# Slots of a graph convolution summed as fp32 column tiles instead of high and low parts, with a third set of row buffers

## The reference

```python
src, dst = (edge_index[0], edge_index[1])          # 100000 edges, sorted by dst
norm = -dinv[src] * dinv[dst]                      # dinv = rsqrt(out-degree)
def _cheb_conv(x, src, dst, norm, W0, W1, b):
    def prop(h):
        return segment_sum(h[src] * norm[:, None], dst, num_segments=x.shape[0])
    return x @ W0 + prop(x) @ W1 + b
...
h = maximum(layernorm(x), 0.0)                     # x: 6250 x 512, fp32
h = _cheb_conv(h, src, dst, norm, W1_0, W1_1, b1)
h = layer_norm(h, gamma, beta)
h = where(h >= 0, h, 0.01 * h)
out = x + _cheb_conv(h, src, dst, norm, W2_0, W2_1, b2)
```

## Time and profile before

| | |
|---|---|
| median of the runs | 2092.93 us |
| profiled execution | span 2091.0 us, from the first to the last instruction; the median lies 1.9 us above it |
| mean granted TensorE clock | 0.980 |
| busy: TensorE, VectorE, ScalarE, GpSimd | 92%, 69%, 72%, 72% |
| DMA | 514.95 MB, 246 GB/s over the span |

### The profile page before, as it was taken

The page is one execution under the profiler, slowest core; times in us unless marked ns, Lnnn a source line. Parts: engine busy times, 40 slices in busy tenths (PEclk is TensorE's granted clock), DMA queues, the critical chain, the costliest instruction groups (busy, mean ns, idle before and its releaser), DMA issues.

```text
span 2091.0 us, 25909 instructions
## 1 busy us (share of the span) xinstructions
PE 1928.9 (92%) x6822; PEld 1074.3 (51%) x6822; DVE 1438.7 (69%) x3415; ACT 1508.8 (72%) x2715; POOL 1511.5 (72%) x1596
## 2 busy tenths in 40 slices
PE   3459999999999999999997999999999999999998
PEld 3435555555555555555554555545555555555545
DVE  9857777877777777877775566655556655556554
ACT  7828788777777888777875776666667666667665
POOL 2267777777777777777777777777777777777775
PEclk9769999999999999999999999999999999999999
DMA  9888888888888888888877888888888888887886
GB/s 251 274 255 274 241 240 241 242 239 239 239 238 238 242 241 240 241 240 236 241 222 252 256 256 260 246 255 254 255 251 248 251 255 254 255 253 240 256 255 183
DMA packets 187921, 514.95 MB, mean 246 GB/s; under 512 B 44460, under 2 KB 46147, under 8 KB 186528
## 3 DMA queue, kind: packets, MB, share of 16 engines
q0 software_dynamic: 128576, 422.78, 68.9%
q1 hardware_dynamic: 56374, 90.16, 12.4%
q10 hardware_dynamic: 2828, 0.42, 0.3%
HBM read 472.40 MB, written 40.84 MB: 245 GB/s over the span
## 4 chain that ended last, share of the span: by engine, by line
PE 49%; POOL 21%; DVE 14%; issue 10%; DMA 6%; ACT 0%; SPq 0%; DVEq 0%; ACTq 0%
PE ps L1313 24%; POOL arena L589 21%; PE ps L1501 11%; PE ps L1494 6%; DMA arena<-table,idx_all 4%; PE ps L1492 4%; DVE low L1092 3%; PE ps L1305 2%; DVE ps L1162 2%; DVE w_all L895 2%; DVE stats L1165 2%; DVE ps L1172 2%; DVE work L895 1%; PE ps L1426 1%; PE ps L1424 1%
## 5 line engine op out<-in xcount | busy, mean ns | idle before, releaser
L589 POOL DMA_INDIRECT arena<-table,idx_all x1536 | 1459.0, 950 | 480.6 <-issue 441.6
L1492 PE MATMUL ps<-high,hots 128*128 128x512 f32 x1034 | 582.0, 563 | 1.4 <-ACT high L699 0.5
L1096 DVE TENSOR_TENSOR low<-arena,ps 128x512 fp32r<-128x512 f32 x517 | 348.5, 682 | 333.7 <-ACT ps L700 329.3
L1501 PE MATMUL ps<-arena,hots_full 128*128 128x512 f32 x1060 | 540.3, 602 | 30.8 <-DMA arena<-table,idx_all 30.1
L700 ACT CAST ps<-arena 128x512 fp32r<-128x512 f32 x517 | 305.1, 590 | 282.2 <-DMA arena<-table,idx_all 251.5
L1494 PE MATMUL ps<-low,hots 128*128 128x512 f32 x1034 | 417.2, 403 | 21.8 <-DVE low L1092 21.8
L1092 DVE SCALAR_TENSOR_TENSOR low<-arena,ps 128x512 fp32r<-128x512 f32 x508 | 366.0, 741 | 66.1 <-ACT ps L699 61.3
L699 ACT ACTIVATE ps<-arena 128x512 fp32r<-128x512 f32 x508 | 348.9, 687 | 31.9 <-DMA arena<-table,idx_all 31.2
L699 ACT ACTIVATE high<-arena 128x512 fp32r<-128x512 f32 x508 | 362.0, 713 | 0.0
L700 ACT CAST high<-arena 128x512 fp32r<-128x512 f32 x517 | 318.5, 616 | 0.0
L1494 PEld LDWEIGHTS ps<-low,hots 128*128 128x128 f32 x1034 | 195.3, 189 | 180.7 <-issue 92.5
(11 more groups left out here) (174 smaller groups left out, 1445.7 us busy)
## 6 DMA issues: line engine op xcount, KB each, us to landing
arena<-table SPq DMA_DIRECT2D x106, 256.0 KB
arena<-table,idx_all POOLq DMA_INDIRECT x1550, 3.9
table<-arena SPq DMA_DIRECT2D x53, 256.0 KB, 4.0
arena<-in_x_dram SPq DMA_DIRECT2D x53, 256.0 KB, 5.3
out_dram<-arena SPq DMA_DIRECT2D x53, 256.0 KB, 4.5
table<-arena SPq DMA_DIRECT2D x10, 1124.4 KB
arena<-in_x_dram POOLq DMA_DIRECT2D x9, 1120.0 KB, 35.2
w_all<-in_L_gnn_W_dram SPq DMA_DIRECT2D x2, 1024.0 KB, 14.4
```

The source lines that it names most:

```text
L589: nc.gpsimd.indirect_dma_start(out=rows[u][0:rn, c, 0:RW if L == 0 else D], out_offset=None, in_=table[L][0:NEAR if near else N, :], in_of ...
L1096: nc.vector.tensor_tensor(low[a], rows[u][:, c, 0:D], high_ps[s % NB][:, :], ALU.subtract).then_inc(s_low, 1)
L1492: nc.tensor.matmul(tx_ps[u][:, :], hot, high[a], start=c == 0, stop=False)
L1501: last = nc.tensor.matmul(tx_ps[u][:, :], hot, rows[u][:, c, 0:D], start=c == 0, stop=i >= NC - 2 and c == SLOTS - 1)
```

## The change

- `SPLIT`, `high`, `low`, `make_high`, `make_low` and the waits that go with them are gone. All slots are plain fp32.
- Each chunk but the last is summed in four strips of 32 nodes: `tx_ps[n % 2][t * 32:(t + 1) * 32]`, from the 32 columns of the hot matrix that belong to strip t. Strip t takes only the slots `STRIPS[t]` that can hold its nodes (0 to 4, 3 to 9, 7 to 13, 10 to 14). The products of different strips are issued in turn. The last chunk of a layer is summed at full width.
- `SETS = 3`: GpSimd fills a set once the chunk three before is summed (`s_tx`), with one wait per chunk.
- The order of all engines is new: a chunk's strips together, then the transposes and dense products. `slots`, `step`, `act_step` and `dve_step` are replaced by `sums`, `sums_last`, `layer_1` and `layer_2`.
- Six edges per chunk (`BOUNDS`) are tested in the prologue: one element of `dst` per slot is loaded on ScalarE's queue, and 24 operations on VectorE compare them with the strips' borders, ahead of the flag.
- SyncE loads own rows of layer 2's first chunks at the end of layer 1.

```diff
-    SPLIT = (0, 1, 4, 6, 7, 9, 10, 12, 13, 14)
...
+    Q = 32
+    STRIPS = ((0, 5), (3, 10), (7, 14), (10, SLOTS))
+    BOUNDS = ((3, False, 1), (5, True, 1), (7, False, 2), (10, True, 2), (10, False, 3), (14, True, 3))
+    ROUNDS = 7
+    SETS = 3
...
+                elif L == 0 and i <= NC - 3:
+
+                    sp.wait_ge(s_t2, i + 3)
+                    sp.wait_ge(s_tab1, 16 * 5)
+                    load_own(1, i - NC + 4)
...
+                    if n >= SETS:
+
+                        pool.wait_ge(s_tx, n - SETS + 1)
                     for c in range(slots_of(i)):
-                        if c % GW == 0 and near:
-
-                            pool.wait_ge(s_slot, summed(0, NC - 1, c + GW - 1))
-                        elif c % GW == 0 and (L or i >= 2):
-
-                            pool.wait_ge(s_slot, summed(L, i - 2, c + GW - 1))
...
+                act.dma_start(slot_edge[:, :, :],
+                              bass.AP(dst.tensor, 0, [[E, 1], [GROUP * P, K // 4], [P, GROUP]])).then_inc(s_bounds, 16)
...
+                copy_own(L, 0)
+                copy_own(L, 1)
+                for i in range(NC):
+                    take_tx(L, i)
+                    if i + 2 < NC:
+                        copy_own(L, i + 2)
+                    copy_txT(L, i)
+                    if L == 0:
+                        take_std(i)
+                        make_sloped(i, i % 2)
...
+                dve.wait_ge(s_bounds, 16)
+                chunk_begin = begin[:, 0:K].rearrange("p (g j) -> p g j", j=4)
+                for n, (c, after_it, strip) in enumerate(BOUNDS):
+                    broken = flags[:, 3 * K + 1 + n * K:3 * K + 1 + (n + 1) * K].rearrange("p (g j) -> p g j", j=4)
+                    for j in range(4):
+                        at = c + (SHORT + (j - 1) * SLOTS if j else 0)
+                        setup.add(nc.vector.scalar_tensor_tensor(
+                            out=broken[:, :, j], in0=chunk_begin[:, :, j], scalar=float(strip * Q),
+                            in1=slot_edge[:, :, at], op0=ALU.add, op1=ALU.is_gt if after_it else ALU.is_le))
...
+            def layer_1():
+                for i in range(NC):
+                    u = i % 2
+                    if i >= 2:
+
+                        dve.wait_ge(s_tx, i - 1)
+                    for c in range(slots_of(i)):
+                        one_hot(0, i, c)
+                        if c == 0 and 1 <= i <= NC - 2:
+                            hot_next(0, i - 1)
...
+                        if i and c == 9:
+                            epi = conv_stats(i - 1, 1 - u)
+                        if i and c == 11:
+                            norm1(i - 1, 1 - u, epi)
+                        if i and c == 13:
+                            finish1(i - 1, 1 - u)
...
+            def layer_2():
+                for i in range(NC):
+
+                    dve.wait_ge(s_tx, NC + i)
                     if i <= NC - 3:
...
+                        hot_next(1, i)
+                    if i + 1 < NC:
+                        for c in range(slots_of(i + 1)):
+                            one_hot(1, i + 1, c)
+                    if i:
+                        finish2(i - 1)
...
+            def strip_sum(L, i, t, c, start, stop):
+                n = L * NC + i
+                strip = slice(t * Q, (t + 1) * Q)
+                return nc.tensor.matmul(tx_ps[n % 2][strip, :], hot_of(n, c)[:, strip], rows_of(n, c)[:, 0:D],
+                                        start=start, stop=stop)
...
+                for r in range(ROUNDS):
+                    if L and i == 0 and r == 4:
+                        add_near(n % 2)
+                    for t in range(4):
+                        c0, c1 = STRIPS[t]
+                        c1 = min(c1, slots_of(i))
+                        c = c0 + r - (t == 3)
+                        if c0 <= c < c1:
+                            if c not in seen:
+                                slot_ready(L, i, c)
+                            seen.add(c)
+                            last = strip_sum(L, i, t, c, c == c0, c == c1 - 1 and not (t == 3 and follows))
+                if follows:
+
+                    pe.wait_ge(s_hotx, L * (NC - 2) + i + 1)
+                    if L:
+                        pe.wait_ge(s_gath[(n + 1) % SETS][0], landed(L, i + 1, 0))
+                    last = nc.tensor.matmul(tx_ps[n % 2][P - Q:P, :], hot_next_of(n), rows_of(n + 1, 0)[:, 0:D],
+                                            start=False, stop=True)
+                last.then_inc(s_tx, 1)
...
+                for i in range(NC):
+                    if i < NC - 1:
+                        sums(L, i)
+                    else:
+                        sums_last(L)
+                    if i + 2 < NC:
+                        transpose_own(L, i + 2)
+                    if i + 1 < NC:
+                        dense_own(L, i + 1)
+                    transpose_tx(L, i)
+                    dense_tx(L, i)
+                    if L == 0 and i in (0, 2):
+                        count_near(i // 2)
```

More of the change, by code:

```diff
@@ L126, in gnn_kernel @@
         gen_rows = arena[0:EP, at_rooms + ROOMS * D:]
[L127 to L132, removed]
+        assert at_own + 7 == ROOMS and at_rooms + ROOMS * D + RW >= NT * RW
+        hots = sb("hots", [P, 2 * SLOTS * P])
+        hots_next = sb("hots_next", [P, 2 * Q])
         w_all = sb("w_all", [P, 2 * KC * D])
@@ L301, in first_slot, with landed, hot_no, own_in @@
             return i // 4 * GROUP + (SHORT + (i % 4 - 1) * SLOTS if i % 4 else 0)
[L303 to L329, removed]
+        def landed(L, i, c):
+            n = L * NC + i
+            return 16 * sum(c < slots_of(m % NC) for m in range(n % SETS, n + 1, SETS))
+        def hot_no(L, i, c):
+            return L * S + first_slot(i) + c + 1
+        def own_in(n):
+            return sum(32 if m < NC else 16 for m in range(n % 2, n + 1, 2))
+        def strips_of(c):
+            return [t for t, (c0, c1) in enumerate(STRIPS) if c0 <= c < c1]
         def scale(i, n):
             return scal[:, bass.ds(i * NSC + n, 1)]
[L336 to L357, removed]
+        def rows_of(n, c):
+            return rows[n % SETS][:, c, :]
+        def hot_of(n, c):
+            at = (n % 2 * SLOTS + c) * P
+            return hots[:, at:at + P]
+        def hot_next_of(n):
+            return hots_next[:, n % 2 * Q:(n % 2 + 1) * Q]
         def products(i, u):
@@ L1455, in dense_own, with transpose_own @@
[L1455 to L1472 removed]
+            def transpose_own(L, i):
+                n = L * NC + i
+                pe.wait_ge(s_ownT, n)
+                pe.wait_ge(s_own[n % 2], own_in(n))
+                transposes(own_ps, own[n % 2]).then_inc(s_t2, 1)
@@ new lines, in dense_own, with dense_tx @@
+            def dense_own(L, i):
+                n = L * NC + i
+                if L and i >= 2:
+                    pe.wait_ge(s_fin, i + 1)
+                else:
+                    pe.wait_ge(s_hs1, n + 1)
+                pe.wait_ge(s_ownT, n + 1)
+                for mm, cols in products(i, n % 2):
+                    last = dense_cols(mm, cols, ownT[n % 2], weights[L][0], True, False)
+                last.then_inc(s_do, 1)
+            def dense_tx(L, i):
+                n = L * NC + i
+                pe.wait_ge(s_txT, n + 1)
+                parts = products(i, n % 2)
+                for k, (mm, cols) in enumerate(parts):
```

407 lines of the change are left out of this document (125 added, 282 removed).

## The result

The changed kernel takes 2082.61 us (2080.64 to 2083.71, 4 runs) against 2092.82 (2092.36 to 2096.65) for the kernel before in the same comparison: a ratio of 0.995, 95% interval 0.9936 to 0.9964. The profiled span went from 2091.0 to 2081.5 us, by 9.5, against the 4.6 forecast.

The account below looks back on a forecast made before the run. GpSimd's gathers, 1.25 us per slot, were taken to bound the kernel before and after. The terms -10.0 + 1.0 + 3.1 + 1.3 gave -4.6 us: span 2086.4, run 2088 us, range 2080 to 2112.

Parts of the forecast that it names:

- What bounds it: Both layers: GpSimd's gathers set the period, 1.25 us per slot, 18.44 us per chunk; TensorE second at about 17 us.
- Strips: TensorE's strip products: four run together, 0.215 us each, so TensorE needs 16 us per chunk against GpSimd's 18.44.
- Rivals 2 and 3: Strip products run in order, 2269 us (chance 0.15), or with no overlap at all, about 3400 us (chance 0.04).
- rival 2: TensorE's strip pairs run in order, 0.43 us per strip, 19.8 to 20.1 us per chunk; 2269 us, chance 0.15.
- Order in layer 1: Layer 1's loop of strips, dense work, epilogue and hots takes 17.5 to 18 us, under 18.44, not holding GpSimd.
- Third set: Start of layer 1: GpSimd's wait at 136 us for chunk 0's row buffer goes, -10.0 us.
- Prologue: Before the gathers: loading slot edges costs +1.0 us (0 to 2.5); the comparisons' 2.2 us before the flag are hidden.
- Gathers: GpSimd's gathers keep 950 ns each whether VectorE is busy or not.
- Transition: Between layers: layer 1's full-width last chunk delays the table's last store, for which GpSimd waits, +3.1 us.
- Tail: End of layer 2: the full-width last chunk's products end at 2083.4 us against 2082.1 before, +1.3 us.
- Clock: TensorE's idle of some 2.7 us per layer 1 chunk may bring 0.50 clock stretches, covered by the wait for gathers.

Follow-up runs that it names:

- experiment 4: Changed kernel with two slots of one strip, then two of the next, in place of one each; 2626.32 us where the changed kernel takes 2618 to 2628.
- Experiment 3: Changed kernel with all products of strip 0, then of strips 1, 2 and 3, instead of the strips in turn; 2807.13 us (one run).
- experiment 1: Changed kernel with two sets of row buffers instead of three; 2096.43 us, ratio 1.0021 to the kernel before.
- experiment 2: Changed kernel without the load of slot edges and the 24 comparisons; 2082.06 us, ratio 0.9954 to the kernel before.
- experiment 5: Changed kernel with all hot matrices made 128 columns wide, products reading the same 32 columns; 2087.08 us, ratio 0.998 to the kernel before.

## Why the prediction was right, step by step

- *What bounds it*: right. GpSimd's pace and slices stayed as they were, and three engines lost work without gain to the run.
- *Strips*: right. Four at once, 0.13 us per instruction: 48 of them, 24 products, took 6.2 us (experiment 4), 3.3 times as fast as at 0.86 us each. Rivals 2 and 3 fell. Experiment 3 shows that they had a mechanism: in another order, the loss of rival 2 and more comes true. The Trainium skill's rule of starts in program order (TensorE: Matmul & The Clock Gate, Part 3, The mechanism), taken strictly for these pairs, does not agree: second instructions start 0.45 us after the first, later strips' firsts 7 ns after.
- *Order in layer 1*: right. The loop was put at 17.5 to 18 us; in the changed kernel's early layer 1, before the gathers hold TensorE up, one chunk's 36 last strip instructions start 17.16 us behind the former's (163.51, 180.67), under GpSimd's 18.44.
- *Third set*: -10.0 forecast, -10.0 measured; experiment 1 gives it 13.8 in the changed kernel, with its one wait per chunk.
- *Prologue*: +1.0 forecast for the load, 0 measured (experiment 2). The flag came 2.5 us later (116.9, for 114.46 in the earlier trace rows; forecast 2.2), but it was needed earlier than at 117.7: GpSimd's queue first loads the flag, 0.5 us from 117.0 on, and only then issues the next gather. So the comparisons cost 0.7.
- *Gathers*: the step that failed. They were taken as fixed at 950 ns; narrow hot matrices made them 3.4 ns shorter each, 5.4 us in all (experiment 5). Wide ones brought 4.5 us back. This term alone is more than the forecast's error of 4.9.
- *Transition*: +3.1 forecast, +1.3 measured. The last chunk's fifteenth gather is issued at 1078.70, and TensorE ends its sums at 1087.2, 8.5 us later; before, it was 7.1.
- *Tail*: +1.3 forecast, +4.2 measured. The 13.7 us of full-width products were as forecast (2058.67 to 2072.4). What came late is all ahead of them: chunk 51's last gather started at 2042.19, landed 5.3 us later and not 3.7, and was summed from 2047.65, and the granted clock was 0.50 from 2047.83 to 2051.24, for part of the dense products at 2049.39, which took 4.62 us for 3.72.
- *Clock*: some stretches at 0.5 came, as in the earlier trace rows; only that last one is seen to cost anything; behind the others GpSimd's pauses are the usual 0.30 us.

The sum was -4.6 and the span moved by -9.5: the start right, the prologue 0.4 too dear, a gain of 5.4 not foreseen, and two errors of the last chunks, -1.8 and +2.9, that half cancel. That the time lies in the range owes something to luck. Its lower end, 2080, stood for a free prologue and cheaper last chunks; the prologue was nearly free, but the last chunks cost 1.1 us more in sum than forecast, and it was the gathers, no part of the range, that took the time to 2082.6.

## What to carry to other kernels

When an engine is off the critical path, taking work from it may still shorten the instructions of the one that is on it: read the spread of the bound engine's durations and what runs beside the long ones, not only their mean. Take apart what a change carries: here the third set of buffers was worth more than the whole gain, and the cleverer products made room for it. And products in separate column tiles overlapped fully here only where they alternated closely in the program, every one or two of a tile.

## What the runs showed of the hardware that was not expected

- Four fp32 products in four tiles of 32 columns run fully side by side, 0.86 us for a round of four pairs. With five to seven of a tile in a row it costs 0.33 us per instruction (experiment 3), with two in a row nothing (experiment 4); a tile seems to have about two products waiting while others start.
- VectorE's hot matrices beside GpSimd's gathers lengthen them, 4 to 5 us over the run for wide ones against narrow ones (experiment 5).
- One chip ran the same program 26% slower (2626.13 against 2082.61), with 540 us of pauses in front of TensorE's weight loads that wait for nothing. A gain of 0.5% on one chip was a loss of 4.5% on another.
